# Tokenizer of a vision tower on one core: matmul operands traded, two tokens side by side, decay products on GpSimd, ScalarE's work in another order

## What is computed

```python
dt  = exp(log_dt); dtA = (-exp(inv_A_real) + 1j * A_imag) * dt[:, None]
Ct  = B[None] * C / (1.0 - dtA / 2) * dt[:, None]
dA_log = log((1.0 + dtA / 2) / (1.0 - dtA / 2))
V   = exp(dA_log[:, :, None] * arange(512))
K   = 2.0 * einsum('chn,hnl->chl', Ct, V).real      # 16 x 256 x 512
```

## Time and profile before

| | us |
|---|---|
| three runs | 1660.93, 1664.78, 1665.66 (median 1664.78) |
| the profiled execution | 1662.74, span 1661.0 |
| tokenizer: start to the last copy out of PSUM | 0 to 222.1 |
| of this, before the first matmul of the loop | 80.2 |
| one turn of the loop | 8.83 |

### The profile page before, as it was taken

How to read it: one execution, slowest core, us unless ns; L and a number is a source line. 1 busy time by engine, 2 the same in 40 slices (tenths; PEclk the granted TensorE clock), 3 DMA queues, 4 the chain that set the end, 5 groups by cost and what they waited for, 6 DMA issues and landing times. The chain is left out here.

```text
span 1661.0 us, 31577 instructions
## 1 busy us (share of the span) xinstructions
PE 1473.0 (89%) x11710; PEld 986.5 (59%) x11710; DVE 1272.4 (77%) x2389; ACT 1002.0 (60%) x2539; POOL 580.4 (35%) x600
## 2 busy tenths in 40 slices
PE   2099967999999999999978888789999599999997
PEld 2099955677766777667756766567665244444443
DVE  8999926777777777777753346269998599999996
ACT  7799916887888877888752224178885233333331
POOL 0000004545445544454530000027777433333332
PEclk9555558999999999999988699989999899999998
DMA  2022252332333233332245037177785244444443
GB/s 83 1 51 64 61 151 84 100 101 94 104 125 102 94 95 105 116 103 98 94 161 178 0 116 241 47 217 206 214 221 137 52 103 101 101 101 102 102 102 83
DMA packets 233098, 183.09 MB, mean 110 GB/s; under 512 B 163568, under 2 KB 164976, under 8 KB 232944
## 3 DMA queue, kind: packets, MB, share of 16 engines
q1 hardware_dynamic: 232944, 181.07, 38.1%
HBM read 93.98 MB, written 59.77 MB: 93 GB/s over the span
## 5 line engine op out<-in xcount | busy, mean ns | idle before, releaser
L1063 PE MATMUL al_ps<-w,al_xT 128*128 128x512 f32 (+2 forms) x1024 | 351.3, 497 | 0.0
L1063 PEld LDWEIGHTS al_ps<-w,al_xT 128*128 128x128 f32 x1024 | 192.2, 193 | 127.1 <-issue 107.3
L2221 POOL TENSOR_TENSOR ff_zq<-ff_z,ff_back 128x1024 bf16<-128x1024 fp8e4 x64 | 122.6, 1915 | 222.9 <-DVE ff_z L2245 222.9
L451 PE MATMUL tk_ps<-tk_w,tk_l 128*128 128x64 f32 x512 | 119.6, 422 | 57.7 <-DVE tk_w L420 50.8
L2187 ACT ACTIVATE ff_sg<-af_ps 128x1024 f32<-128x1024 f32 x64 | 65.5, 1024 | 150.7 <-PE af_ps L2270 150.7
L451 PEld LDWEIGHTS tk_ps<-tk_w,tk_l 128*128 128x128 f32 x512 | 114.2, 332 | 60.3 <-issue 60.3
L756 POOL TENSOR_TENSOR al_qv<-al_qv,al_qe 128x512 f32<-128x512 f32 x48 | 63.2, 1316 | 219.8 <-PE al_ps L1126 219.8
L2270 PE MATMUL af_ps<-wgT,xqT 128*128 128x512 bf16 x512 | 122.7, 383 | 13.6 <-ACT ff_sg L2187 13.6
L2291 PE MATMUL af_ps<-wdT,ff_zT 128*128 128x512 bf16 x512 | 123.9, 386 | 5.9 <-DMA ff_zT<-ff_zq 5.9
L2270 PE MATMUL af_ps<-wuT,xqT 128*128 128x512 bf16 x512 | 122.1, 381 | 6.8 <-DVE ff_z L2237 4.8
L2042 PE MATMUL af_ps<-ag_w,ag_aT 128*128 128x512 f32 x256 | 112.6, 593 | 1.7 <-ACT af_ps L1878 1.7
(11 more groups left out here) (299 smaller groups left out, 3388.8 us busy)
## 6 DMA issues: line engine op xcount, KB each, us to landing
al_hx<-h_s SPq DMA_DIRECT2D x36, 256.0 KB, 2.7
o_s<-al_o SPq DMA_DIRECT2D x32, 272.0 KB, 2.2
h_s<-tk_w SPq DMA_DIRECT2D x16, 512.0 KB, 3.8
v_s<-al_v SPq DMA_DIRECT2D x32, 256.0 KB, 2.3
k_s<-al_kT SPq DMA_DIRECT2D x32, 256.0 KB, 2.3
q_s<-al_qT SPq DMA_DIRECT2D x32, 256.0 KB, 2.7
lt_k<-k_s SPq DMA_DIRECT2D x16, 512.0 KB, 5.0
lt_v<-v_s SPq DMA_DIRECT2D x16, 512.0 KB, 3.7
```

Source lines behind the costliest of these rows:

```text
L451: ins = pe.matmul(o, L[:, u, 0, t], R[:, u, t], start=True, stop=t < CS)
L1063: ins = pe.matmul(out, xT[:, T, k], w[:, k, cols], start=False, stop=True, skip_group_check=True)
L2221: pool.tensor_tensor(zq[:, u].rearrange("p (k s) -> p k s", s=QB), z8[:, u].rearrange("p (k s) -> p k s", s=QB), back[:, u, :, None].to_br ...
```

## The change

**Loop, TensorE.** The operands trade places: `R` (64 columns) becomes the weights and `L` (128 columns) moves. An even token writes to partitions 0 to 63 of PSUM, the odd one to 64 to 127 of the same columns. Real and imaginary part are always summed in PSUM, so there are 32 matmuls per turn instead of 19, and L417 goes. The result lies the wrong way round, so ACT copies it to `mid` (`turned`), TensorE turns it in 8 transposes of 128x128 (`turns`) and ACT copies again (`tokens`).

**Loop, GpSimd.** It takes the product into `R` (L420 before) and a raw phase product (`raw`), which replaces the 16 small activations L254; one activation of 128x1024 adds the offset (`phases`). `R` now waits for all of `ER`.

**Preparation.** GpSimd makes the 8 products of `ER`, in the order 4, 5, 0, 1, 2, 3, 6, 7, since the first four blocks share memory with `xdup`. ACT does 6 groups of X, the Exp of `WA`, phases and rounding of turn 0, 4 groups, the two Sin of `W`, 6 groups, then the 8 Exp. DVE makes the fraction of turn 0 before the products with `WA`.

```diff
@@ scalar @@
             def phases(ch):
-                if ch >= 2:
-                    act.wait_ge(nf_ready, ch - 1)
-                for t in range(CH):
-                    ins = act.activation(ph[:, ch % 2, t], c("iota_a"), ACT.Identity,
-                                         scale=par[:, 1, ch * CH + t:ch * CH + t + 1], bias=c("off_r"))
-                ins.then_inc(ph_ready, 1)
+                act.wait_ge(raw_ready, ch + 1)
+                act.activation(ph[:, ch % 2], ph[:, ch % 2], ACT.Identity, bias=c("off_r")).then_inc(ph_ready, 1)
...
+            def turned(ch):
+                act.wait_ge(mm_ready, ch + 1)
+                if ch >= 2:
+                    act.wait_ge(tr_ready, ch - 1)
+                for k in range(2):
+                    ins = act.activation(mid[:, ch % 2, 4 * k:4 * k + 4], ps[ch % 2 * 2 + k][:].rearrange(
+                        "p (j q) -> p j q", j=4), ACT.Copy)
+                ins.then_inc(mid_ready, 1)
             def tokens(ch):
-                act.wait_ge(mm_ready, ch + 1)
+                act.wait_ge(tr_ready, ch + 1)
...
+            turned_x(range(6))
+            act.wait_ge(s_wph, 1)
+            act.activation(WA, WA, ACT.Exp).then_inc(s_wa, 1)
             phases(0)
             rounded(0)
+            turned_x(range(6, 10))
+            for w in range(2):
+                act.wait_ge(s_wph, 2 + w)
+                act.activation(W[:, w], W[:, w], ACT.Sin, scale=-TWO_PI, bias=tau[:, 1 + w:2 + w]).then_inc(s_wsn, 1)
+            turned_x(range(10, 16))
+            decays()
             for ch in range(NCH):      # Sin(ch), phases(ch + 1), rounded(ch + 1), then:
                 if ch:
-                    tokens(ch - 1)
+                    turned(ch - 1)
+                if ch >= 2:
+                    tokens(ch - 2)
@@ gpsimd, new @@
+            def raw(ch):
+                if ch >= 2:
+                    pool.wait_ge(nf_ready, ch - 1)
+                t0 = ch * CH
+                pool.tensor_tensor(ph[:, ch % 2], par[:, 1, t0:t0 + CH, None].to_broadcast([P, CH, 64]),
+                                   c("iota_a")[:, None, :].to_broadcast([P, CH, 64]), ALU.mult).then_inc(raw_ready, 1)
+            raw(0)
+            for k in DECAY:
+                t0 = 32 * k
+                if k == 0:
+                    pool.wait_ge(s_xtr, 16)
+                pool.tensor_tensor(ER[:, t0:t0 + 32], par[:, 0, t0:t0 + 32, None].to_broadcast([P, 32, 64]),
+                                   c("iota_a")[:, None, :].to_broadcast([P, 32, 64]), ALU.mult).then_inc(s_er0, 1)
+            pool.wait_ge(s_pb, 1)
+            for ch in range(NCH):
+                t0, u = ch * CH, ch % 2
+                if ch + 1 < NCH:
+                    raw(ch + 1)
+                pool.wait_ge(sin_ready, ch + 1)
+                pool.wait_ge(s_er, 8)
+                if ch >= 2:
+                    pool.wait_ge(mm_ready, ch - 1)
+                pool.tensor_tensor(R[:, u], nf[:, u], ER[:, t0:t0 + CH], ALU.mult).then_inc(r_ready, 1)
@@ vector, loop @@
-                dve.tensor_tensor(L[:, u, 0, 0:CS], L[:, u, 0, 0:CS], L[:, u, 1, 0:CS], ALU.add).then_inc(l_ready, 1)
-                dve.wait_ge(sin_ready, ch + 1)
-                dve.wait_ge(s_er, ch // 2 + 1)
-                dve.tensor_tensor(R[:, u], nf[:, u], ER[:, t0:t0 + CH], ALU.mult).then_inc(r_ready, 1)
@@ tensor @@
+            def turns(ch):
+                pe.wait_ge(mid_ready, ch + 1)
+                if ch >= 2:
+                    pe.wait_ge(hs_ready, ch - 1)
+                for j in range(PAIRS):
+                    ins = pe.transpose(ps[4 + ch % 2 * 2 + j // 4][:, (j % 4) * P:(j % 4) * P + P],
+                                       mid[:, ch % 2, j], ident)
+                ins.then_inc(tr_ready, 1)
             for ch in range(NCH):
...
+                for j in range(PAIRS):
+                    for k in range(2):
+                        for half in range(2):
+                            t = 2 * j + half
+                            ins = pe.matmul(ps[u * 2 + j // 4][64 * half:64 * half + 64, (j % 4) * P:(j % 4) * P + P],
+                                            R[:, u, t], L[:, u, k, t], start=k == 0, stop=k == 1)
                 ins.then_inc(mm_ready, 1)
+                if ch:
+                    turns(ch - 1)
+            turns(NCH - 1)
```

More of the change, by code:

```diff
@@ L120, in tokenizer @@
     CH = 16
-    CS = 13
+    PAIRS = CH // 2
+    DECAY = (4, 5, 0, 1, 2, 3, 6, 7)
     NCH = TOK // CH
@@ L151, in tokenizer @@
                  for k in range(2))
+        mid = nat[:, 0:16].rearrange("p k a n -> p (k a n)").rearrange("p (u j q) -> p u j q", u=2, j=PAIRS)
         ps = [ctx.enter_context(nc.psum_tensor(f"tk_ps{i}", [P, 512], F32)) for i in range(8)]
@@ L178, in tokenizer @@
         s_wsn = sem("tk_wsn")
+        s_wa = sem("tk_wad")
         s_pb = sem("tk_pbd")
+        raw_ready = sem("tk_raw_ready")
+        mid_ready = sem("tk_mid_ready")
+        tr_ready = sem("tk_tr_ready")
         ph_ready = sem("tk_ph_ready")
@@ L233, in _, with turned_x, decays @@
                     ins.then_inc(s_xd, 1)
[L234 to L247, removed]
-            def phases(ch):
-                if ch >= 2:
-                    act.wait_ge(nf_ready, ch - 1)
-                for t in range(CH):
-                    ins = act.activation(ph[:, ch % 2, t], c("iota_a"), ACT.Identity,
-                                         scale=par[:, 1, ch * CH + t:ch * CH + t + 1], bias=c("off_r"))
-                ins.then_inc(ph_ready, 1)
+            def turned_x(ks):
+                for k in ks:
+                    ri, q, a = k // 8, k % 4, (k % 8) // 4
+                    act.wait_ge(s_xtr, k + 1)
+                    act.activation(X[:, ri, a * P:(a + 1) * P, 4 * q:4 * q + 4],
+                                   ps[(k + 2) % 8][:].rearrange("p (q t) -> p t q", q=4), ACT.Copy).then_inc(s_ev, 1)
+            def decays():
+                for n, k in enumerate(DECAY):
+                    act.wait_ge(s_er0, n + 1)
+                    act.activation(ER[:, 32 * k:32 * k + 32], ER[:, 32 * k:32 * k + 32], ACT.Exp).then_inc(s_er, 1)
+            def phases(ch):
+                act.wait_ge(raw_ready, ch + 1)
+                act.activation(ph[:, ch % 2], ph[:, ch % 2], ACT.Identity, bias=c("off_r")).then_inc(ph_ready, 1)
             def rounded(ch):
@@ L270, in tokens @@
                 for k in range(2):
-                    ins = act.activation(hs[:, ch % 2, 8 * k:8 * k + 8], ps[ch % 2 * 2 + k][:].rearrange(
+                    ins = act.activation(hs[:, ch % 2, 8 * k:8 * k + 8], ps[4 + ch % 2 * 2 + k][:].rearrange(
                         "p (t a) -> p t a", t=8), ACT.Copy)
                 ins.then_inc(hs_ready, 1)
-            act.wait_ge(s_xd, 4)
-            act.wait_ge(s_par, 2)
+            turned_x(range(6))
+            act.wait_ge(s_wph, 1)
+            act.activation(WA, WA, ACT.Exp).then_inc(s_wa, 1)
             phases(0)
             rounded(0)
+            turned_x(range(6, 10))
[4 more added lines that the diff above has]
+            decays()
             for ch in range(NCH):
@@ L286, in _ @@
                 if ch:
-                    tokens(ch - 1)
-            tokens(NCH - 1)
+                    turned(ch - 1)
+                if ch >= 2:
+                    tokens(ch - 2)
+            tokens(NCH - 2)
+            turned(NCH - 1)
+            tokens(NCH - 1)
+        @block.gpsimd
+        def _(pool):
+            def raw(ch):
[4 more added lines that the diff above has]
+                                   c("iota_a")[:, None, :].to_broadcast([P, CH, 64]), ALU.mult).then_inc(raw_ready, 1)
+            pool.wait_ge(s_ld, 80)
+            pool.wait_ge(s_xd, 4)
+            pool.wait_ge(s_par, 2)
+            raw(0)
[15 more added lines that the diff above has]
+                pool.tensor_tensor(R[:, u], nf[:, u], ER[:, t0:t0 + CH], ALU.mult).then_inc(r_ready, 1)
         @block.vector
@@ L380, in _, with fractions @@
                                          ).then_inc(s_wph, 1)
[L381 to L386, removed]
+            def fractions(ch):
+                dve.wait_ge(rr_ready, ch + 1)
+                dve.scalar_tensor_tensor(nf[:, ch % 2], nf[:, ch % 2], ROUND, ph[:, ch % 2], ALU.subtract, ALU.subtract
+                                         ).then_inc(nf_ready, 1)
+            fractions(0)
+            dve.wait_ge(s_wa, 1)
             for w in range(2):
+                dve.wait_ge(s_wsn, w + 1)
                 st(dve.tensor_tensor(W[:, w], W[:, w], WA, ALU.mult))
@@ L398, in _ @@
             dve.wait_ge(s_ev, 16)
[L400 to L406, removed]
             for ch in range(NCH):
@@ L411, in _ @@
                 for k in range(2):
[L412 to L416, removed]
-                dve.tensor_tensor(L[:, u, 0, 0:CS], L[:, u, 0, 0:CS], L[:, u, 1, 0:CS], ALU.add).then_inc(l_ready, 1)
-                dve.wait_ge(sin_ready, ch + 1)
-                dve.wait_ge(s_er, ch // 2 + 1)
```

(16 more changed lines are left out.)

## The result

The changed kernel takes 1683.1 us (median of four runs, 1678.4 to 1685.1), the kernel before 1665.2 beside it: ratio 1.0101, 95% interval 1.0083 to 1.0119, slower by 18 us. The forecast was 1686.

What follows compares the result with a forecast made beforehand. DVE, nearly full, bounds turn and preparation, and shares one resource with GpSimd: preparation +11.5, turns +9.0, last turn's missing `raw` -1.6, tail +2.2, sum +21.1 us to 1683.8, plus 2.0 to the median: 1686; 8-in-10 range 1652 to 1712.

Steps and rivals of the forecast that it cites:

- DVE and GpSimd as one resource: Preparation and loop: two-SBUF-input DVE instructions and GpSimd products alternate, so their times add, less 0.14 us per handover.
- Rival A: Preparation and loop: long DVE products don't wait for GpSimd; 1655 at 1.2 GHz (11%), 1608 at 2.4 GHz (8%).
- Turn: Loop: DVE's 5.72 plus GpSimd's 4.27, less handovers, gives 9.43 us against 8.83; +9.0 over fifteen turns.
- The saving of 0.28 per GpSimd instruction: Preparation and loop: handovers hide instruction starts, 0.56 us saved a turn and 2.5 in preparation.
- Decay product: Preparation: a GpSimd product of 2048 elements takes 3.64 us by the spread-operand line, 4.52 by the other.
- Preparation: Before the loop: DVE and GpSimd work adds to 61.0 us, `Pb` at 83.5, first matmul at 91.7, +11.5 us.
- TensorE: the price: Loop matmuls: 64 half-width records at half the full-width price, about 0.107 us each at 1.2 GHz; 6.9 us a turn.
- B: Loop matmuls: array halves don't overlap with 128 moving columns; 15.9 us a turn at 1.2 GHz, 1792 in all, 4%.
- the 0.4 for two changes of form: TensorE's turn: two switches of array form between matmuls and transposes cost an estimated 0.4 us.
- Tail: After the last `R`: longer chain of transposes and copies, +4.7 us at 1.2 GHz, -0.2 at 2.4; +2.2 taken.
- What PE waits for: Loop: PE would show idle time before each turn, waiting for GpSimd's `R`.
- 16 x 0.425 - 1.15: Loop, ACT: sixteen small activations replaced by one large one, put at 5.2 us saved; about 5.5 left a turn, free.

Runs made afterwards that it cites:

- e3: Changed kernel with `R`, `raw` and the decay products all on DVE, GpSimd without a program in this stage: 1648.1 us, ratio 0.9908.
- e4: Changed kernel with ScalarE copying each turn's x to PSUM, where DVE's long products read it; one pair of banks fewer for second transposes: 1637.1 us.
- e5: Changed kernel with each of the loop's two GpSimd products replaced by two memsets, so GpSimd only writes there: 1624.5 us, ratio 0.9775.
- e8: Changed kernel with one wait altered, so the next turn's `raw` waits for this turn's fraction: 1679.4 us, ratio 1.0105.
- e7: Changed kernel with x slices read from PSUM, decay products on DVE, and next `raw` waiting for this turn's fraction: 1612.1 us, ratio 0.9708.

## Why the prediction was right, point by point

- **DVE and GpSimd as one resource: right, for what stands in this stage.** Shown by e3, e4 and e5, not by the changed kernel's trace alone. Rival A is out: a long product waits as the one of 128x32 did.
- **Turn: 9.43 forecast, 9.42 measured.** The saving of 0.28 per GpSimd instruction holds for long ones too. The rule that the other engine blocks for the whole instruction, "Who interferes with whom" in "SBUF — State Buffer" of the Trainium skill, taken to the letter, would have given 9.99. What the Trainium skill says there of two-input DVE instructions beside GpSimd's readers and writers agrees with e4 and e5 in the loop.
- **Decay product: 3.64 forecast, 7.29 / 2 = 3.65 measured.** The line through the spread form was the right one.
- **Preparation: `Pb` at 83.5 forecast, 83.44 measured; first matmul 91.7 and 91.97.** The way there was not as told. I had all nine GpSimd instructions alternate with DVE and the last phase factor at 62 to 64; it was ready at 47.3 (41.74 + 5.59). GpSimd stood idle for 8.96 us before block 0: DVE's product for `WA` was held to 33.87, so ScalarE made its Exp, and with it copies 6 to 9 of x, late, and TensorE's last transposes waited for those. It cost nothing, since DVE ran free meanwhile: it is busy 60.64 of the 61.02 us from 22.45 to 83.47, so the sum does not hang on the order. The Exps ended at 74.2, so ScalarE had 9 us to spare, where I saw none.
- **TensorE: the price was right, so B is out; its reason is open.** 64 records in 3.71 at 2.4 GHz are (3.71 - 0.27) / 63 = 0.055 each, 0.062 forecast; in the first turn, at a granted clock of 0.55, (6.58 - 0.41) / 63 = 0.098, 0.107 forecast for 1.2 GHz (0.27 and 0.41 are the means of one record there). That both halves work at once is not shown: by the prediction's own rows the load of 128 weight columns set the full price, and half as many weight columns could halve it without any overlap. The transposes start 3.64 after their block does, so the 0.4 for two changes of form does not show.
- **Tail: the mis-sized term.** +2.2 taken between the two clock levels, -0.4 measured: TensorE was at 2.4 GHz there (granted clock 1.00 from 231.5 to 240.7), for which the prediction had -0.2. That is most of the 3 us between forecast and median. The reason given for a higher clock, denser streaming, is not shown by any run.
- **What PE waits for: half wrong.** I named GpSimd's `R`; in the steady turns it is DVE's second product, which GpSimd's `R` had held. In e8, where `raw` comes later, it is `R`. The waits of the changed kernel, from 94 to 230:

```profile
PE tk_ps L511 <- DVE tk_l L464: 48.1, 14, 4.7
POOL tk_w L344 <- ACT tk_xin L301: 33.7, 14, 4.5
```

- **A slip without effect: ACT.** 16 x 0.425 - 1.15 is 5.65 and not 5.2. By the group's busy time (86.3 / 16 = 5.39) ACT loses 4.2 and gains 1.1 of its 8.48, so 5.3; measured is 5.19, far below the turn.

## What to carry to other kernels

Before moving work from VectorE to GpSimd, count the SBUF inputs of what stays: beside a GpSimd product a two-input VectorE product stands still, and the price is the sum of both, with GpSimd's 1.6 to 2 times VectorE's for the same product. Give the VectorE product one operand in PSUM and the move pays (here 9.42 to 6.49 us a turn for a copy of 0.58). The number of inputs is not the whole test: TENSOR_SCALAR from SBUF to SBUF, with one input, waited too (4.63 for 1.29 in e4), even for a memset in e5. A busy share won't show the wait: compare the mean of one form before and after.

## What the runs showed that I had not expected

TensorE's clock in the loop. Before, PE was busy 95% of a turn and the granted clock stood at 0.50 in the turns of the earlier trace rows, and at 5 in all slices of the loop in the earlier trace rows. After, it is busy for 4.7 to 7.5 us of a turn of 9.42, yet the turns read 0.68 to 0.93. One of them:

```profile
139.00:148.42 9.42, 4.74 (x72) 4.36 (x72) 9.42 (x4) 5.19 (x7) 7.17 (x3) 0.85 0.27 68
```

The blocks of 64 records take between 3.71 and 6.58 us in the changed kernel, after 1.3 to 4.7 us of idle time; in e4 and e7, after 0.8 to 2 us, they take 3.7 once the first is past, and a turn reads 1.00. Before, the same engine streamed 64 columns past 128 weight columns; now it streams 128 past 64, with transposes and idle time between the blocks. Which of these differences lifts the clock was not separated.

A later stage that the change does not touch takes its own time from run to run: from the start of the first to that of the last record of L1522 (L1584 after) it is 67.9 us before, 71.2 after, and 66.1 to 73.4 over all ten profiled executions. A difference of 3 us between two medians of this program can come from there; the first matmul and the turn, read from the trace, are steadier than the time.
